# A graph layer on one core: other waits of the gathers and scatters, and normalisation in 30 chunks 1658 rows apart with a last piece of 256 rows

## The reference

```
w   = MLP(radial_embedding(edge_length))            # per edge, 4 x 32
xs, xv = x[:, :32] @ W_up0, x[:, 32:] @ W_up1       # per node
ss, vv = xs[src], xv[src]                           # gather by sender
mid = products of w, ss, vv and the edge's direction
msg = segment_sum(mid, dst, 50000)                  # add by receiver
out = x + (msg @ W_out) / 16
out = (out - mean(out)) / sqrt(var(out) + 1e-5)     # per row
```

## Time and profile before

| | |
|---|---|
| median of 3 runs | 1323.9 us |
| the profiled execution | 1335.3 us |
| its span | 1333.5 us |
| GpSimd busy | 1014.3 us (76%) |
| TensorE busy | 928.8 us (70%) |
| VectorE busy | 692.2 us (52%) |
| ScalarE busy | 537.5 us (40%) |
| moved by DMA | 130.36 MB, mean 98 GB/s |

### The profile page before, as it was taken

The page is one execution under the profiler, slowest core; times in us unless marked ns, Lnnn a source line. Parts: engine busy times, 40 slices in busy tenths (PEclk is TensorE's granted clock), DMA queues, the critical chain, the costliest instruction groups (busy, mean ns, idle before and its releaser), DMA issues.

```text
span 1333.5 us, 25760 instructions
## 1 busy us (share of the span) xinstructions
PE 928.8 (70%) x6206; PEld 871.6 (65%) x6206; DVE 692.2 (52%) x2882; ACT 537.5 (40%) x1403; POOL 1014.3 (76%) x817
## 2 busy tenths in 40 slices
PE   2577688787788867776876768777876766767800
PEld 1477577787677766766776767676776766767700
DVE  5364334465576456556556466465465556555402
ACT  5233233244445534444444444434443434534301
POOL 6347878888888888888888888888888888888761
PEclk7588877887888889889879897788788888898955
DMA  4377786433443443453453453443444444443332
GB/s 131 113 184 161 168 185 120 94 65 67 114 97 67 93 116 69 90 119 69 90 120 67 91 118 69 93 110 73 94 92 91 94 92 93 93 91 68 59 28 63
DMA packets 82548, 130.36 MB, mean 98 GB/s; under 512 B 16168, under 2 KB 66763, under 8 KB 81232
## 3 DMA queue, kind: packets, MB, share of 16 engines
q0 software_dynamic: 68992, 51.43, 28.7%
q1 hardware_dynamic: 12888, 77.27, 17.3%
q10 hardware_dynamic: 632, 1.29, 0.3%
HBM read 78.31 MB, written 77.22 MB: 117 GB/s over the span
## 4 chain that ended last, share of the span: by engine, by line
issue 31%; POOL 28%; DMA 11%; PE 8%; another core or an unknown queue 7%; SPq 5%; ACT 4%; POOLq 3%; ACTq 1%; DVE 0%; DVEq 0%
POOL acc L444 20%; POOL sender L420 7%; DMA acc<-msg,index 6%; DMA acc<-in_x_dram 5%; SPq L295 3%; PE ps_msg L553 2%; PE ps_sum L541 2%; ACT normed L693 2%; PE ps_wts L528 2%; POOLq L427 1%; PE ps_hid L512 1%; PE ps_dst L494 1%; PE ps_sT L500 1%; ACT hid L656 1%
## 5 line engine op out<-in xcount | busy, mean ns | idle before, releaser
L444 POOL DMA_INDIRECT acc<-msg,index x392 | 621.1, 1585 | 170.3 <-issue 111.0
L420 POOL DMA_INDIRECT sender<-in_x_dram,index x392 | 386.8, 987 | 123.5 <-issue 111.9
L541 PE MATMUL ps_sum<-same,mid 128*128 128x128 f32 x1568 | 248.0, 310 | 1.5 <-issue 0.8
L541 PEld LDWEIGHTS ps_sum<-same,mid 128*128 128x128 f32 x1568 | 240.3, 226 | 10.0 <-DVE mid L930 0.8
L915 DVE TENSOR_TENSOR wts<-ps_wts,bias 128x512 f32<-128x512 f32 x98 | 67.8, 692 | 323.2 <-PE ps_wts L528 205.4
L528 PE MATMUL ps_wts<-mlp,hid 128*128 128x128 f32 x784 | 139.4, 335 | 104.9 <-ACT hid L668 100.6
L632 ACT COPY sumT<-ps_sum 128x512 f32<-128x512 f32 x196 | 114.9, 587 | 235.5 <-remote 131.3
L553 PE MATMUL ps_msg<-outw,sumT 128*128 128x64 f32 x1568 | 202.0, 285 | 2.3 <-ACT sumT L632 1.6
L553 PEld LDWEIGHTS ps_msg<-outw,sumT 128*128 128x128 f32 x1568 | 200.0, 206 | 3.2 <-issue 1.2
L528 PEld LDWEIGHTS ps_wts<-mlp,hid 128*128 128x128 f32 x784 | 126.6, 245 | 111.8 <-ACT hid L668 107.0
L512 PE MATMUL ps_hid<-hid,mlp 128*128 128x256 f32 x196 | 78.8, 490 | 150.2 <-ACT hid L656 110.1
(11 more groups left out here) (135 smaller groups left out, 1061.5 us busy)
## 6 DMA issues: line engine op xcount, KB each, us to landing
acc<-in_x_dram SPq DMA_DIRECT2D x80, 312.5 KB
total<-acc SPq DMA_DIRECT2D x30, 832.0 KB
out_dram<-normed SPq DMA_DIRECT2D x29, 832.0 KB
sender<-in_x_dram,index POOLq DMA_INDIRECT x392
acc<-msg,index POOLq DMA_INDIRECT x392
out_dram<-normed ACTq DMA_DIRECT2D x1, 832.0 KB
vec_raw<-in_edge_attr_dram SPq DMA_DIRECT2D x1, 576.0 KB
acc<-zeros SPq DMA_DIRECT2D x1, 320.0 KB, 3.9
```

The costliest lines, as they stand in the source:

```text
L420: pool.indirect_dma_start(sender[:, u % SRING, i, :], None, x, bass.IndirectOffsetOnAxis(ap=index[:, u, 0, i:i + 1], axis=0)).then_inc(gat ...
L444: pool.indirect_dma_start(acc, bass.IndirectOffsetOnAxis(ap=index[:, v, 1, i:i + 1], axis=0), msg[:, v % RING, i, :], None, compute_op=ALU.add
L541: mm = pe.matmul(ps_sum[r][:, i, h, :], mid[:, b, 2 * r + i, P * h:P * (h + 1)], same[:, b, 2 * r + i, :], start=True, stop=True)
```

## The change

Four things change. The waits of a scatter: scatter n, counted over all units, waits for the landing of scatter n-3 always, and for n-1 (scatter 0 of a unit: n-2 and n-1) only if `meets` is 1; `meets` now compares each tile with the two before it over all units. The waits of a gather: gather i of unit u waits for gather i of unit u-1, on semaphores of its own; TensorE waits for each gather ahead of its transpose. The order of the four tiles in a unit: both of one row of edges, then both of the other. The chunks: still 1664 rows, but 1658 apart, so that they overlap by six rows; each store waits for the store before; up to 30 may be final in the loop; the last piece is rows 0 to 255 in two rows per partition.

```diff
+STEP = CHUNK - 6
+CHUNKS = 30
+REST_ROWS = 2
+REST = P * REST_ROWS
 ...
-        meet = sb("meet", [1, UNITS, G * (G - 1) // 2])
+        meet = sb("meet", [1, 2, TILES])
 ...
-            return a.rearrange("p (j w) (q r) -> p w q j r", w=2, r=2)[:, w]
+            return a.rearrange("p (j w) (r q) -> p w q j r", w=2, r=2)[:, w]
 ...
             def store(h, b):
                 c = 2 * h + b
                 sp.wait_ge(normed_ready, c + 5)
+                sp.wait_ge(stored[1 - b], 16 * h + 16 + 16 * b)
 ...
-            done = sp.value_load(done_count[0:1, 0:1], min_val=0, max_val=CHUNKS - 1)
+            done = sp.value_load(done_count[0:1, 0:1], min_val=0, max_val=CHUNKS)
+            half = sp.value_load(done_half[0:1, 0:1], min_val=0, max_val=CHUNKS // 2 - 1)
             with sp.If(done % 2):
-                load(done // 2, 1)
-            with sp.If(CHUNKS - 1 - done):
+                load(half, 1)
+            with sp.If(CHUNKS // 2 - (done + 1) // 2):
 ...
-            sp.dma_start(total[0:REST, CHUNKS % 4, 0, :], acc[0:REST, :]).then_inc(total_in[0], 16)
+            sp.dma_start(total[:, CHUNKS % 4, 0:REST_ROWS, :].rearrange("p r d -> p (r d)"),
+                         acc[0:REST, :].rearrange("(p r) d -> p (r d)", p=P)).then_inc(total_in[0], 16)
 ...
+            pool.memset(meet[:, :, :], 0.0)
 ...
+            def landed(n):
+                return slot_done[n // G % 2][n % G], 16 * (n // G // 2) + 32
+            def here(u, i):
+                return (slot_done[u][i], 16) if u < 2 else (gathered[u % 2][i], 16 * (u // 2))
             def gathers(u):
-                if u >= 2:
-                    pool.wait_ge(gathered[u % 2], 16 * G * (u // 2))
 ...
                 for i in range(G):
+                    if u >= 1:
+                        pool.wait_ge(*here(u - 1, i))
 ...
             def scatters(v):
 ...
-                if v >= 1:
-                    for i in range(G):
-                        pool.wait_ge(scattered[1 - c][i], 16 * ((v + 1) // 2))
                 for i in range(G):
-                    if i >= 1:
-                        if v >= 2:
-                            pool.wait_ge(scattered[c][i - 1], 16 * (v // 2) + 16 * meets)
-                        else:
-                            pool.wait_ge(scattered[c][i - 1], 16)
+                    n = G * v + i
+                    if n >= 3:
+                        pool.wait_ge(*landed(n - 3))
+                    for of in (n - 2, n - 1) if i == 0 else (n - 1,):
+                        if of >= 0:
+                            to, count_after = landed(of)
+                            pool.wait_ge(to, count_after - 16 + 16 * meets)
 ...
-                pe.wait_ge(gathered[b], u * (16 * G // 2) + 16 * G - 16 * G * b // 2)
 ...
                 for i in range(G):
+                    if k < 2:
+                        pe.wait_ge(slot_done[b][i], 16)
+                    else:
+                        pe.wait_ge(gathered[b][i], 8 * (u - b))
                     mm = pe.transpose(ps_sT[:, P * i:P * (i + 1)], sender[:, k % SRING, i, :], ident[:, :])
 ...
+                for apart in range(1, 3):
+                    n = TILES - apart
+                    dve.tensor_tensor(meet[:, apart - 1, apart:TILES], hi[:, 0:n], lo[:, apart:TILES], ALU.is_ge)
+                    mm = dve.tensor_tensor(meet_too[:, apart - 1, apart:TILES], hi[:, apart:TILES], lo[:, 0:n], ALU.is_ge)
 ...
-                link(dve.tensor_scalar(rising[:, :], rising[:, :], float(CHUNKS - 1), None, ALU.min))
+                link(dve.tensor_scalar(rising[:, :], rising[:, :], float(CHUNKS), 0.0, ALU.min, ALU.max))
 ...
-                    dve.tensor_copy(done_count[:, k:k + 1], final[:, PAIRS - after:PAIRS - after + 1])
+                    done = final[:, PAIRS - after:PAIRS - after + 1]
+                    dve.tensor_copy(done_count[:, k:k + 1], done)
+                    link(dve.tensor_scalar(done_odd[:, k:k + 1], done, float(CHUNKS - 1), None, ALU.min))
+                    dve.tensor_scalar(done_half[:, k:k + 1], done_odd[:, k:k + 1], -0.5, 0.5, ALU.add, ALU.mult)
```

More of the change, by code:

```diff
@@ L208, in bass_gnn @@
         sp_passed = sem("sp_passed")
-        gathered = [sem(f"gathered{b}") for b in range(2)]
+        gathered = [[sem(f"gathered{b}_{i}") for i in range(G)] for b in range(2)]
         basis_staged = sem("basis_staged")
@@ L234, in bass_gnn @@
         msg_ready = sem("msg_ready")
-        scattered = [[sem(f"scattered{b}_{i}") for i in range(G)] for b in range(2)]
+        slot_done = [[sem(f"slot_done{b}_{i}") for i in range(G)] for b in range(2)]
         total_in = [sem(f"total_in{b}") for b in range(2)]
@@ L682, in _, with normalise @@
             act.sem_inc(normed_ready, 4)
-            def normalise(h, b, part, rows=ROWS, parts=P, store=False):
+            def normalise(h, b, part, rows=ROWS, store=False):
                 c = 2 * h + b
@@ L692, in normalise @@
                 for r in (range(half, rows) if part else range(half)):
[L693 to L696, removed]
+                    mm = act.activation(normed[:, b, r, :],
+                                        total[:, quarter, r, :].rearrange("p b d -> p (b d)"), ACT.Identity,
+                                        scale=rstd[:, b, r:r + 1], bias=shift[:, b, r:r + 1])
+                if part == 0:
                     return
@@ L729, in _ @@
             unit(UNITS, UNITS, tail=True)
[L730 removed]
+            done = act.value_load(done_count[0:1, 2:3], min_val=0, max_val=CHUNKS)
+            half = act.value_load(done_half[0:1, 2:3], min_val=0, max_val=CHUNKS // 2 - 1)
             with act.If(done % 2):
                 for part in range(2):
[L733 to L734 removed]
+                    normalise(half, 1, part, store=True)
+            with act.If(CHUNKS // 2 - (done + 1) // 2):
                 with act.Fori((done + 1) // 2, CHUNKS // 2) as h:
@@ L738, in _ @@
                             normalise(h, b, part, store=True)
-            normalise(CHUNKS // 2, 0, 0, 1, REST, store=True)
+            for part in range(2):
+                normalise(CHUNKS // 2, 0, part, REST_ROWS, store=True)
         @block.vector
@@ L943, in moments, with statistics @@
                 for r in range(rows):
-                    mm = dve.bn_stats(stats[0:parts, r, :], total[0:parts, quarter, r, :].rearrange("p b d -> p (b d)"))
+                    mm = dve.bn_stats(stats[:, r, :], total[:, quarter, r, :].rearrange("p b d -> p (b d)"))
                 mm.then_inc(stats_ready, 1)
-            def statistics(h, b, rows=ROWS, parts=P):
+            def statistics(h, b, rows=ROWS):
                 c = 2 * h + b
-                st = stats[0:parts, 0:rows, :]
-                mn, hg, gs = (a[0:parts, 0:rows] for a in (mean, half_gap, gap_sq))
-                vr, rs, sh, bt = (a for a in (var[0:parts, 0:rows], rstd[0:parts, b, 0:rows],
-                                              shift[0:parts, b, 0:rows], bits[0:parts, 0:rows]))
+                st = stats[:, 0:rows, :]
+                mn, hg, gs, vr, bt = (a[:, 0:rows] for a in (mean, half_gap, gap_sq, var, bits))
+                rs, sh = (a[:, b, 0:rows] for a in (rstd, shift))
                 step = SSTEPS * c
@@ L1000, in _ @@
             pair(PAIRS - 1, UNITS - 2, last=True)
-            done = dve.value_load(done_count[0:1, 1:2], min_val=0, max_val=CHUNKS - 1)
+            done = dve.value_load(done_count[0:1, 1:2], min_val=0, max_val=CHUNKS)
+            half = dve.value_load(done_half[0:1, 1:2], min_val=0, max_val=CHUNKS // 2 - 1)
             with dve.If(done % 2):
-                moments(done // 2, 1)
-                statistics(done // 2, 1)
-            with dve.If(CHUNKS - 1 - done):
+                moments(half, 1)
+                statistics(half, 1)
+            with dve.If(CHUNKS // 2 - (done + 1) // 2):
                 with dve.Fori((done + 1) // 2, CHUNKS // 2) as h:
```

53 lines of the change are left out of this document (25 added, 28 removed).

## The result

| | kernel before | changed kernel |
|---|---|---|
| time, median (range) | 1323.8 (1321.33 to 1324.72, 4 runs) | 1280.38 (1277.2 to 1281.76, 4 runs) |
| profiled execution, span | 1335.3, 1333.5 | 1277.2, 1275.0 |
| message 0 done | 67.38 | 48.80 |
| scatter 0 of unit 2 | 110.78 | 75.10 |
| last scatter | 1307.45 | 1260.84 |

The ratio is 0.9671, 95% interval 0.9647 to 0.9695: 43.4 us faster, where 35.9 were forecast (1288, range 1280 to 1304).

The account below looks back on a forecast made before the run. GpSimd's own issue was taken to set the pace, so only its idle places could gain: 14.5 + 13.5 + 9.4 - 1.5 = 35.9 us off the 1323.9 median, giving 1288 us, range 1280 to 1304.

Parts of the forecast that it names:

- case A: Whole kernel: gains at head, last units and tail less one new cost, 1288 us, own range 1281 to 1295; chance 0.76.
- the three places: Where GpSimd stands idle: the head, the last six units, after the last scatter; gains 14.5, 13.5 and 9.4 us.
- Units 0 and 1: Head: landing stalls of scatters 1 to 3, 17.2 us, go; 14.5 us gained, ends 9 and 17.2.
- Units 92 to 97: Last six units: each first scatter no longer waits for the previous unit's last; 13.5 us gained, ends 11 and 13.5.
- After the last scatter: Tail: chunk 29 done in the loop, only the 256-row piece remains; 26.05 us becomes 16.7, gain 9.4.
- The new wait for n-3: A unit's fourth scatter waits for its first, 5.67 us earlier; cost 1.5 us, none at best, 15 at worst.
- no idle over 0.5 at fourth scatters: Expected sign in GpSimd's timeline that each unit's fourth scatter is not held by the first one's landing.
- Rival C: Mid-run: fourth scatters wait on landings; restart 6.2 us gives 1335; chance 0.05 for slower, 0.03 for a milder form.
- Gathers, the memset of `meet`, `meet`'s rows, the new order of tiles: Possible side costs on GpSimd, VectorE and transfers: hidden or the same bytes, nothing charged.
- Rival D: Tail: chunk 29 not final in time, 256-row piece behind it, about 1 us longer than before; 1298 us, chance 0.04.
- B: Head: late messages of units 2 to 12 give the gain back, leaving 0 to 7; 1295 to 1303 us, chance 0.12.
- the milder form of C: Mid-run: restart of 5.8 us makes fourth scatters' waits cost 12 us, 1298 us; chance 0.03.

Follow-up runs that it names:

- head-undone run: Changed kernel with scatters 1 to 3 of units 0 and 1 again waiting for the landing of the one ahead: 1299.41 us, ratio 0.9811.
- all old waits: Changed kernel with the earlier waits of scatters and gathers; chunks, tile order and TensorE's waits as changed: 1314.7 us, ratio 0.9921.
- the kernel before with its message held up: Kernel before with eleven more ScalarE copies ahead of unit 0's first Silu: 1344.6 us; the same copies in the changed kernel: 1299.53 us.
- second chip: Chip of set 2, both kernels run again unchanged: kernel before 1336.83 us (1337.74 as the set's base), changed kernel 1304.14 us, ratio 0.9759.
- pairs: Profiles of kernel before against changed kernel: first profiles, second chip (33.6 us faster), and both with eleven extra ScalarE copies delaying message 0 (1344.6 and 1299.53 us).
- window of two: Changed kernel with every scatter waiting for the landing of the one two ahead, in place of three: 1375.96 us, ratio 1.039.
- third chip: Chip of set 3, changed kernel run again unchanged as base: 1281.49 us, ratio 0.9672, against 1326.61 us for the kernel before.

## Why the prediction came out as it did

The forecast, case A, named the three places and the one new cost, and each place is shown by undoing it: 19.0 us for the head, 19.4 for the last units as they lie now, 9.7 for the chunks without the new waits. These three don't add up (48.1 for 43.4), since the wait of the last units costs more beside the last chunk's store, and since each is good to about 4 us only. The mechanism was right and the sum too small by 7.5 us: 1280.38 lies 0.6 below case A's own range of 1281 to 1295 and 0.4 inside the whole one of 1280 to 1304. What was missed are sizes:

- **Units 0 and 1**, 14.5 forecast. The stall was taken as 17.2 from one profile and cut by 2.7 for VectorE's longer `make_dense_orders` and for message leads of 17.0. Neither decided in the result: `make_dense_orders` with the product behind it did grow, from 9.32 to 10.20 us (0.9; 1.2 forecast), but the smallest lead left was 3.6 us. And the stall is larger where restarts run to 6.0: 20.2 in the head-undone run, 21.2 with all old waits, 19.7 in the kernel before with its message held up, and 17.2 and 16.6 in the two profiles of the kernel before with "remote" waits. (With an early first message the kernel before itself was never profiled.) That is the largest miss, some 5 us. The leads of 17 belonged to a profile whose messages ran slowly, as on the second chip; there the stretch up to unit 6 gained 10.3 (13.9-3.6). The gap of 11.4 between that profile and its median had been noted, and subtracting the same gain from both was the choice that failed: the head differs between the two.
- **Units 92 to 97**, 13.5 forecast, 12.1 to 12.9 in the pairs. Chunk 29's load costs one idle of 0.85. The step held for the change as a whole; undone alone it costs more, as above.
- **After the last scatter**, 9.4 forecast, 11.8 to 12.3. SyncE's issue came at 5.28 (5.4 taken), the statistics and their chain took 3.7 (0.5+3.4 taken), the two activations 0.9, the store's issue 0.03 behind them (0.3 taken), but the 128 KB load took 2.15 and not 2.8, and from the store to the end it was 2.1 (1275.0-1272.87) and not 3.4. Both had been taken from between rows of transfers that were larger or had others beside them; here the load and the store each stood alone. The Trainium skill, "DMA: Bandwidth & Descriptors", section "Anatomy of one DMA — SWDGE (gpsimd) path", whose fit is for transfers issued by GpSimd, would give an estimated 2.3 us for 128 KB: the 2.15 of this load, which SyncE issued, fits, while for 832 KB it says 3.95 and the row has 4.73 (1234.44 to 1239.17). The prediction stayed with the rows for both, and was right for the long one only. It said that the rule would lower the sum by 1 us at most; taken for the store too it is 1.6 (0.5+1.1).
- **The new wait for n-3**, 1.5 forecast. Five idles exceed 0.35 us, four at fourth scatters between 131 and 171 us and one at 1240, together 1.8 beyond the ordinary gap. The sign "no idle over 0.5 at fourth scatters" was missed by three of them (0.56 to 0.83). Rival C was rightly small, but nearer than the mid-run rows showed: in the run with the window of two a restart there takes 4.6 to 4.7 in the mean and up to 6.0, and the window is 5.67.
- **Gathers, the memset of `meet`, `meet`'s rows, the new order of tiles**: nothing forecast. The prediction said that a gather's stall in the head would cost its length if GpSimd's idle of 20.5 us went; it went (0.86 in the result). The gathers idled 0.6 us there and 3.3 on the third chip. The scatter tables ended 0.9 us later (26.29 for 25.37) behind another wait, GpSimd's first gather at 11.71 for 11.61, a mid-run unit 12.74 for 12.72.
- **Rival D** did not occur: chunk 29 was loaded at 1234.44.
- **The chances**: A, B, D and the milder form of C sum to 0.95, not to the 0.92 stated for "faster"; C's 0.03 were counted in both places.

What bounds the kernel now: from 49.76 to 1260.84 GpSimd issues 391 scatters of 1.60 and 364 gathers of 0.975 with 0.30 behind each, 742.9+464.1 = 1207.0 of 1211.1 us. More can be gained only by fewer or shorter issues, an earlier first scatter or a shorter end. An earlier message alone gives little: the last of the 28 gathers ahead of the first scatter ends at 48.90, so at most 0.56 us (49.76-49.20) would come of it, and nothing in the third chip's profile; the gathers must come earlier too. None of the variants run here beats the changed kernel.

## What to carry to other kernels

Before a gain in time is worked out from a trace, ask whether that execution is a typical one: where its own time lies 11 us off the median, find the stretch that differs, look for waits that other profiles lack, and size the steps there from both sides. A wait for a transfer's landing is free only while the issue work between the two is longer than the landing at its worst beside other traffic; here a window of 5.67 us cost 1.8 us over the run and one of 3.85 cost 96. Work that follows the last result is best split so that all but the smallest piece is final early: moving one chunk of 30 into the loop was worth 9.7 us on its own, although the piece left over grew from 80 to 256 rows.

## What the runs showed of the hardware

- A restart behind a scatter's landing depends on what moves beside it: 4.1 to 4.4 us in the quiet end, 4.6 to 4.7 in the mean of mid-run and up to 6.0 (window of two), 4.1 to 6.4 beside the 312.5 KB copies, 6.5 beside an 832 KB store.
- The same program ran at 1280 and 1281 us in two sets and at 1304 in a third, on another chip, the kernel before at 1324 to 1327 and at 1337 to 1338. All four profiles of the slower set have 629 to 714 us of waits with the releaser "remote" on ScalarE and VectorE together, the profile of before 561, the other nine none. In the changed kernel's profile from that set, ScalarE and VectorE do nothing from 40.0 to 52.4 us, and TensorE 0.02 us, while GpSimd goes on. Whether the chip or the time of the runs makes it is open.
